# One scale per token instead of scaled copies: the norms of cross attention and router, and the last additions

## What is computed

```python
x = _layernorm(x + _L0_attn_ref(x, ...))        # rotary self attention, softmax and linear memory mixed by a gate
x = _layernorm(x + _L0_xattn_ref(x, ctx, ...))  # cross attention on 64 context tokens
x = _layernorm(x + _L0_ffn_ref(x, ...))         # 64 experts, 8 per token, 64 slots each
# inside the cross attention:
x = rmsnorm(hidden_states, norm_w)              # x * rsqrt(mean(x*x) + 1e-6) * norm_w
q = x @ wq.T
attn = softmax(q k^T * HD**-0.5)                # HD = 16, masked context tokens left out
out = (attn v) @ wo.T
return sigmoid(x @ wg.T) * out
# inside the experts:
probs = softmax(x @ gate_w.T); w, sel = top_k(probs, 8)
```

## Time and profile before

| | us |
|---|---|
| median of 3 runs (453.71 to 455.42) | 454.6 |
| the profiled execution | 454.77 |
| its span in the trace | 453.0 |
| PE busy, share of the span | 292.5 (65%) |
| DVE busy | 226.3 (50%) |
| POOL busy | 168.8 (37%) |
| ACT busy | 129.3 (29%) |

### The profile page before, as it was taken

The page is one execution under the profiler, slowest core; times in us unless marked ns, Lnnn a source line. Parts: engine busy times, 40 slices in busy tenths (PEclk is TensorE's granted clock), DMA queues, the critical chain, the costliest instruction groups (busy, mean ns, idle before and its releaser), DMA issues.

```text
span 453.0 us, 5276 instructions
## 1 busy us (share of the span) xinstructions
PE 292.5 (65%) x1732; PEld 184.2 (41%) x1732; DVE 226.3 (50%) x509; ACT 129.3 (29%) x238; POOL 168.8 (37%) x172
## 2 busy tenths in 40 slices
PE   4475767598996798977889648730059999760000
PEld 3352534455655466564365424620035545330000
DVE  0826451567447766377713624132037777430694
ACT  1340354116652156531355113100014443230000
POOL 1300030300302762118700067105705568484662
PEclk9885699869999699996999659765569999975555
DMA  7299998980075230572200199200059999955951
GB/s 273 89 181 290 358 386 212 234 286 1 1 163 117 104 127 2 135 144 83 79 2 1 55 275 300 57 23 8 1 161 265 317 225 190 247 64 96 359 200 46
DMA packets 44829, 69.75 MB, mean 154 GB/s; under 512 B 5851, under 2 KB 30041, under 8 KB 44034
## 3 DMA queue, kind: packets, MB, share of 16 engines
q1 hardware_dynamic: 36688, 59.67, 45.3%
q0 software_dynamic: 7680, 9.47, 10.3%
q10 hardware_dynamic: 434, 0.27, 0.3%
HBM read 42.74 MB, written 31.90 MB: 165 GB/s over the span
## 4 chain that ended last, share of the span: by engine, by line
PE 39%; DVE 18%; DMA 17%; issue 10%; ACT 6%; POOL 5%; SPq 2%; POOLq 0%; DVEq 0%; ACTq 0%
PE M L1000 16%; PE O L1000 11%; DMA acc_d<-xp_t,idx_out 9%; PE SA L1000 4%; PE SB L1000 4%; DMA early<-part_d 4%; DVE nmax L741 3%; DVE early L980 3%; POOL xin_d L440 2%; ACT xp_t L555 2%; DMA part_d<-early 2%; PE M L1172 2%; DVE xn L894 2%; SPq L340 1%; PE M L1035 1%
## 5 line engine op out<-in xcount | busy, mean ns | idle before, releaser
L440 POOL DMA_INDIRECT xin_d<-row,idx_slot x64 | 62.9, 983 | 28.8 <-issue 18.8
L484 POOL DMA_INDIRECT acc_d<-xp_t,idx_out x32 | 49.5, 1548 | 35.1 <-DVE idx_out L951 13.4
L466 POOL TENSOR_TENSOR early<-early 128x1024 f32<-128x1024 f32 x4 | 8.5, 2131 | 86.0 <-ACT early L543 86.0
L426 POOL TENSOR_SCALAR rstd<-mv 128x2 f32<-128x2 f32 x8 | 1.8, 222 | 92.5 <-DVE mv L719 92.5
L1000 PE MATMUL O<-probs,early 128*32 128x256 f32 x256 | 32.8, 385 | 4.2 <-ACT probs L533 2.2
L1000 PE MATMUL SA<-early 96*128 96x256 bf16 (+1 forms) x128 | 23.2, 313 | 12.0 <-DMA early<-part_d 5.6
L1000 PE MATMUL SB<-early 96*128 96x256 bf16 (+1 forms) x128 | 23.1, 311 | 5.1 <-DVE nmax L741 4.8
L1330 PE MATMUL O<-con,probs 128*128 128x128 f32 x40 | 9.2, 320 | 26.2 <-DMA probs<-xin_d 26.2
L741 DVE TENSOR_REDUCE nmax<-SB 128x4 f32<-128x1024 f32 x16 | 19.5, 1219 | 10.8 <-PE SB L1000 10.8
L741 DVE TENSOR_REDUCE nmax<-SA 128x4 f32<-128x1024 f32 x16 | 19.5, 1217 | 10.4 <-PE SA L1000 10.4
L1000 PE MATMUL O<-xf,early 128*128 128x256 f32 x64 | 19.5, 462 | 5.3 <-DMA early<-weights 5.3
(11 more groups left out here) (190 smaller groups left out, 649.3 us busy)
## 6 DMA issues: line engine op xcount, KB each, us to landing
gu_sb<-wgu SPq DMA_DIRECT2D x21, 384.0 KB, 7.8
acc_d<-zeros SPq DMA_DIRECT2D x3, 2176.0 KB, 19.7
early<-acc_d SPq DMA_DIRECT2D x24, 256.0 KB, 5.8
xin_d<-zeros SPq DMA_DIRECT2D x1, 5136.0 KB, 24.5
early<-wgu SPq DMA_DIRECT2D x11, 384.0 KB, 11.0
wd_sb<-wd SPq DMA_DIRECT2D x21, 192.0 KB, 8.4
early<-part_d SPq DMA_DIRECT2D x28, 128.0 KB, 7.2
probs<-xin_d SPq DMA_DIRECT2D x20, 160.5 KB, 4.7
```

Of the source, the lines that this page charges most:

```text
L440: nc.gpsimd.indirect_dma_start(xin_d, bass.IndirectOffsetOnAxis(ap=idx_slot[:, t, k:k + 1], axis=0), row[:, t, :], None, bounds_check=SLOT ...
L466: nc.gpsimd.tensor_tensor(rest[:], qk[:], parts[:, :, 0], ALU.subtract).then_inc(S["rest_r"], 1)
L484: nc.gpsimd.indirect_dma_start(acc_d[p % CHAINS], bass.IndirectOffsetOnAxis(ap=idx_out[:, p:p + 1], axis=0), yw[:, p % YRING, :], None, bo ...
```

## The change

The scaled copies go. PE transposes `res` itself, before any norm: for cross attention instead of `xn`, for the router instead of `row`. What the norm would have done is put elsewhere:

- The mean: once, at the end of the first iteration, a new `folded` multiplies `w_xq` and `w_xg` by the norm weight and subtracts from them and from the router weights their column mean, which PE forms with a matrix of 1/256 (`mean_of`).
- The scale: POOL makes three scales per token in `nrm` (for the router, for the exponential with the factor 1/4, for the tanh with the factor 1/2), two more adds and one power of six columns. ACT takes them as the scale of its exponentials and of the tanh, which becomes two instructions. For the router DVE multiplies the maximum by `rstd` (`lbias`).
- `x1` is still written for the residual, now behind `score_max(0)`; the rows are written in a new `rows`, behind `router_max`.
- The final stage: POOL's addition goes. DVE adds three parts to three in one instruction of 768 columns, then two of 256; the steps of three tiles are interleaved. ACT does the normalisation (Identity with scale and bias), DVE makes its bias (`fshift`).

```diff
-        rstd = sb("rstd", [P, NT])
+        nrm = sb("nrm", [P, 3, NT])
+        rstd = nrm[:, 0]
+        mean_of = sb("mean_of", [P, P])
         x1 = sb("x1", [P, NT, D])
-        sq = sb("sq", [P, NT, D])
-        ssum = sb("ssum", [P, NT])
-        rinv = sb("rinv", [P, NT])
-        xn = sb("xn", [P, NT, D])
-        xn_f = sb("xn_f", [P, NC, T])
+        x1_f = sb("x1_f", [P, NC, T])
...
+            nc.gpsimd.memset(mean_of[:], 1.0 / D).then_inc(S["setup"], 1)
...
-                passed(pool)
-                nc.gpsimd.tensor_scalar(rstd[:], mv[:, :, 1], 1e-5, None, ALU.add).then_inc(S["var"], 1)
-                need(pool, "var", b, ln)
-                nc.gpsimd.tensor_tensor(rstd[:], rstd[:], mhalf[:, 0:NT], ALU.pow).then_inc(S["rstd"], 1)
+                    prev(pool, "xexp", b)
+                    prev(pool, "eprob", b)
+                    nc.gpsimd.tensor_scalar(nrm[:, 1], mv[:, :, 1], HD * (1.0 + 1e-6), HD * 1e-11, ALU.mult, ALU.add
+                                            ).then_inc(S["var"], 1)
+                    nc.gpsimd.tensor_scalar(nrm[:, 2], mv[:, :, 1], 4.0 * (1.0 + 1e-6), 4e-11, ALU.mult, ALU.add
+                                            ).then_inc(S["var"], 1)
+                nc.gpsimd.tensor_scalar(rstd, mv[:, :, 1], 1e-5, None, ALU.add).then_inc(S["var"], 1)
+                need(pool, "var", b, 2 + ln)
+                if ln == 1:
+                    nc.gpsimd.tensor_tensor(nrm[:].rearrange("p k t -> p (k t)"), nrm[:].rearrange("p k t -> p (k t)"),
+                                            mhalf[:, 0:3 * NT], ALU.pow).then_inc(S["rstd"], 1)
+                else:
+                    nc.gpsimd.tensor_tensor(rstd, rstd, mhalf[:, 0:NT], ALU.pow).then_inc(S["rstd"], 1)
...
-                    need(pool, "sq", b)
-                    prev(pool, "xn", b)
-                    passed(pool)
-                    nc.gpsimd.tensor_scalar(rinv[:], ssum[:], 1.0 / D, 1e-6, ALU.mult, ALU.add).then_inc(S["ssum"], 1)
-                    need(pool, "ssum", b)
-                    nc.gpsimd.tensor_tensor(rinv[:], rinv[:], mhalf[:, 0:NT], ALU.pow).then_inc(S["rinv"], 1)
...
-            def final_half(t):
-                pool.wait_ge(S["gu"][t], fin_base[t] + 16 * CHAINS)
-                by_two = fin[:, t].rearrange("p (c h) d -> p c h d", h=2)
-                nc.gpsimd.tensor_tensor(by_two[:, 1:, 0], by_two[:, 1:, 0], by_two[:, 1:, 1], ALU.add).then_inc(S["fpool"], 1)
-            final_half(0)
             for t in range(TILES):
-                if t + 1 < TILES:
-                    final_half(t + 1)
                 pool.wait_ge(S["fmv"], t + 1)
-                nc.gpsimd.tensor_scalar(rstd[:, t % 2:t % 2 + 1], mv[:, t % 2, 1:2], 1e-5, None, ALU.add).then_inc(S["fvar"], 1)
+                nc.gpsimd.tensor_scalar(frstd[:, t:t + 1], fmv[:, t, 1:2], 1e-5, None, ALU.add).then_inc(S["fvar"], 1)
                 pool.wait_ge(S["fvar"], t + 1)
-                nc.gpsimd.tensor_tensor(rstd[:, t % 2:t % 2 + 1], rstd[:, t % 2:t % 2 + 1], mhalf[:, 0:1],
-                                        ALU.pow).then_inc(S["frstd"], 1)
+                nc.gpsimd.tensor_tensor(frstd[:, t:t + 1], frstd[:, t:t + 1], mhalf[:, 0:1], ALU.pow).then_inc(S["frstd"], 1)
...
-                    nc.scalar.activation(xp[:, t], xp[:, t], ACT.Exp, scale=HD ** -0.5).then_inc(S["xexp"], 1)
+                    nc.scalar.activation(xp[:, t], xp[:, t], ACT.Exp, scale=nrm[:, 1, t:t + 1]).then_inc(S["xexp"], 1)
...
-                    need(act, "lmax", b)
+                    need(act, "lbias", b)
+                    need(act, "rstd", b)
                     for t in range(NT):
                         nc.scalar.activation(eprob[:, t], M[:, 1, t * E:(t + 1) * E], ACT.Exp,
-                                             bias=lmax[:, t:t + 1]).then_inc(S["eprob"], 1)
...
-                        nc.scalar.activation(sq[:, t], x1[:, t], ACT.Square, accum_out=ssum[:, t:t + 1]).then_inc(S["sq"], 1)
-                    need(act, "xn_mm", b)
-                    for n in range(NC):
-                        nc.scalar.activation(xn_f[:, n], M[:, 0, n * T:(n + 1) * T], ACT.Copy,
-                                             scale=par[:, NH + n:NH + n + 1]).then_inc(S["xn_ev"], 1)
+                                             bias=lbias[:, t:t + 1], scale=nrm[:, 0, t:t + 1]).then_inc(S["eprob"], 1)
+                if b is not None:
+                    need(act, "x1_mm", b)
+                    nc.scalar.activation(x1_f[:].rearrange("p c t -> p (c t)"), M[:, 0, :], ACT.Copy).then_inc(S["x1_ev"], 1)
...
-                    nc.scalar.activation(sgate[:].rearrange("p t d -> p (t d)"), gate_place(a), ACT.Tanh, scale=0.5
-                                         ).then_inc(S["gate_th"], 1)
+                    need(act, "rstd", b, 1)
+                    for t in range(NT):
+                        nc.scalar.activation(sgate[:, t], gate_place(a)[:, t * D:(t + 1) * D], ACT.Tanh, scale=nrm[:, 2, t:t + 1]
+                                             ).then_inc(S["gate_th"], 1)
...
+            for t in range(TILES):
+                act.wait_ge(S["fshift"], t + 1)
+                act.wait_ge(S["frstd"], t + 1)
+                nc.scalar.activation(fin[:, t, 0], fin[:, t, 0], ACT.Identity, scale=frstd[:, t:t + 1], bias=fshift[:, t:t + 1]
+                                     ).then_inc(S["fout"], 1)
...
+            def folded():
+                dve.wait_ge(S["w_in"], 16 * 7)
+                dve.wait_ge(S["par_in"], 16)
+                for w in ("xq", "xg"):
+                    for c in range(NC):
+                        nc.vector.tensor_scalar(w_sb[w][:, c], w_sb[w][:, c], par[:, NH + c:NH + c + 1], None, ALU.mult
+                                                ).then_inc(S["fold"], 1)
+                dve.wait_ge(S["fold"], 2 * NC)
+                dve.wait_ge(S["fold_mm"], 1)
+                for i, w in enumerate(("xq", "xg")):
+                    nc.vector.tensor_tensor(w_sb[w][:], w_sb[w][:], M[:, 1, i * D:(i + 1) * D].unsqueeze(1).broadcast_to([P, NC, D]),
+                                            ALU.subtract).then_inc(S["fold"], 1)
+                nc.vector.tensor_tensor(router_sb[:], router_sb[:], M[:, 0, 0:E].unsqueeze(1).broadcast_to([P, NC, E]),
+                                        ALU.subtract).then_inc(S["fold"], 1)
...
+                    statistics(b, 2)
+                def rows():
...
-                    statistics(b, 2)
                     normalized(b, 2, row, "x2")
...
+                    need(dve, "lmax", b)
+                    need(dve, "rstd", b)
+                    nc.vector.tensor_tensor(lbias[:], lmax[:], rstd, ALU.mult).then_inc(S["lbias"], 1)
...
+                if a is not None:
+                    score_max(0)
                 if b is not None:
                     normalized(b, 1, x1, "x1")
-                if a is not None:
-                    score_max(0)
-                if b is not None:
-                    need(dve, "rinv", b)
-                    prev(dve, "xn_mm", b)
-                    for t in range(NT):
-                        nc.vector.tensor_scalar(xn[:, t], x1[:, t], rinv[:, t:t + 1], None, ALU.mult).then_inc(S["xn"], 1)
...
                 if b is not None:
                     router_max()
+                    rows()
                     route()
                 if a is not None:
...
+                if b is None and a is None:
+                    folded()
...
-            def total(t):
+            def halves_added(t):
                 dve.wait_ge(S["gu"][t], fin_base[t] + 16 * CHAINS)
-                f = fin[:, t]
-                nc.vector.tensor_tensor(f[:, 0], f[:, 0], f[:, 1], ALU.add).then_inc(S["fadd"], 1)
-                dve.wait_ge(S["fpool"], t + 1)
-                for c in range(1, CHAINS):
-                    dve.wait_ge(S["fadd"], CHAINS * t + c)
-                    nc.vector.tensor_tensor(f[:, 0], f[:, 0], f[:, 2 * c], ALU.add).then_inc(S["fadd"], 1)
-                dve.wait_ge(S["fadd"], CHAINS * (t + 1))
-                nc.vector.bn_stats(stats[:, t % 2], f[:, 0]).then_inc(S["fstat"], 1)
+                nc.vector.tensor_tensor(fin[:, t, 0:3], fin[:, t, 0:3], fin[:, t, 3:6], ALU.add).then_inc(S["fpair"], 1)
+            def thirds_added(t, c):
+                dve.wait_ge(S["fpair"], t + 1)
+                if c == 2:
+                    dve.wait_ge(S["fadd"], 2 * t + 1)
+                nc.vector.tensor_tensor(fin[:, t, 0], fin[:, t, 0], fin[:, t, c], ALU.add).then_inc(S["fadd"], 1)
...
+            def row_stats(t):
+                dve.wait_ge(S["fadd"], 2 * t + 2)
+                nc.vector.bn_stats(fstats[:, t], fin[:, t, 0]).then_inc(S["fstat"], 1)
...
-                nc.vector.bn_aggr(mv[:, t % 2], stats[:, t % 2]).then_inc(S["fmv"], 1)
...
+                nc.vector.bn_aggr(fmv[:, t], fstats[:, t]).then_inc(S["fmv"], 1)
...
-                nc.vector.tensor_scalar(fin[:, t, 0], fin[:, t, 0], mv[:, t % 2, 0:1], rstd[:, t % 2:t % 2 + 1],
```

(37 more changed lines are left out.)

41 lines of the change are left out of this document (22 added, 19 removed).

## The result

| | before | after |
|---|---|---|
| median, us | 455.01 (4 runs, 453.71 to 455.72) | 438.67 (4 runs, 436.04 to 443.70) |
| ratio | | 0.9615, 95% interval 0.9567 to 0.9663 |
| profiled execution, span | 454.77, 453.0 | 443.70, 441.9 |
| batch 3's first residual to its `idx_slot` | 50.8 | 48.9 |
| first addition to last normalisation | 26.1 | 21.4 |

The change makes the kernel 3.9% faster. The forecast of 436.2 was 2.5 us low; the range (430.5 to 443.0) holds the median. The trace of after is that of the slowest of its four runs, which the ratio leaves out: it shows 11.1 us of gain in the span where the forecast had 18.6 and the median 16.3. A run of 437.3, that of half_scatters (experiment 6), is put beside it further down.

What follows compares the result with a forecast made beforehand. It took the last iteration's chain through every norm step, and DVE at borders and final stage, as the bound. 1.0 - 2.6 - 8.7 + 0.3 - 4.2 - 4.4 = -18.6, from 454.77 to 436.2 us; range 430.5 to 443.0.

Steps and rivals of the forecast that it cites:

- beginning, to the first maximum: First iteration: `folded`'s work on PE and DVE outlasts a transfer wait and delays the first maximum; +1.0 us.
- borders, to batch 3's first residual: Three borders with self attention beside: DVE sets the pace and writes `x1` in place of `xn`; -2.6 us.
- last iteration, front, to the scores: Last iteration, residual to context scores: PE at the full clock, POOL's `xk_blk` arriving last; -8.7 us.
- behind the scores, to the second residual: Last iteration, ACT: the tanh becomes two instructions, with the exponentials behind it on the path; +0.3 us.
- router, to `route`: Last iteration, second residual to `route`: PE starts at once, at the full clock; -4.2 us.
- experts, to the first addition: Experts' stage, 305 to 421 us: not touched, only starting earlier by what is won before; 0.
- final stage, to the last normalisation: Final stage: without POOL's addition a tile costs DVE 2.4 us, before 3.26; -4.4 us.
- The first rival: Borders: PE's clock stays high once its wait for `xn` is gone; 431.7 us in all, chance 0.13.
- fourth rival: New pauses keep PE at 1.2 GHz; slower than before from 18.6 us of such work, 473 at twice that; chance 0.04.

Runs made afterwards that it cites:

- experiment 6: Changed kernel with every second of POOL's 16 scatters of the first three batches left out: 437.9 us (436.3 to 444.6), ratio 0.9623.
- pval_again: Changed kernel with PE's wait for `pval` moved behind the transposes, in a series where the kernel before took 475.1: 451.9 us, ratio 0.9505.
- pval_calm: Changed kernel with PE's wait for `pval` moved behind the transposes, in an undisturbed series: 437.3 us (434.9 to 440.4), ratio 0.9636.
- filled_calm: pval_calm plus a few matmuls nobody reads in PE's pauses of the last iteration, same series: 431.1 us (430.5 to 433.8), ratio 0.9504.
- the two disturbed series: First two of four measurement series, everything 4% longer: the kernel before took 474.4 and 475.1 us, against 454.5 and 454.4 in the last two.

## Why the prediction was right, and where not

The sum was -18.6, the median's gain 16.3. The terms, by two traces: that of after (a run of 443.7) and that of half_scatters (a run of 437.3, the same kernel but for half of the scatters of the first three batches). Change against before, us:

| term | forecast | run of 443.7 | run of 437.3 |
|---|---|---|---|
| beginning, to the first maximum | +1.0 | +1.18 | +0.86 |
| borders, to batch 3's first residual | -2.6 | -4.39 | -3.30 |
| last iteration, front, to the scores | -8.7 | -5.88 | -6.43 |
| behind the scores, to the second residual | +0.3 | +7.79 | +0.35 |
| router, to `route` | -4.2 | -3.83 | -3.54 |
| experts, to the first addition | 0 | -0.86 | +0.72 |
| final stage, to the last normalisation | -4.4 | -4.67 | -6.32 |
| end | 0 | -0.44 | +0.16 |
| sum | -18.6 | -11.1 | -17.5 |

- *Beginning.* The work of `folded` was hidden in after and cost 0.4 in pval_again. Its matmuls took 0.55 + 1.08 + 1.03 in after and not the 4.8 of the low clock, because the clock was up. The first maximum is nevertheless 1.18 later than before: the operands landed later (38.30 against 37.12), as did everything since the first transfers. That is not the change, so the +1.0 was met by accident.
- *Borders.* First to second maximum shrank from 3.49, 4.06, 4.06 to 3.00, 3.00, 3.01: -2.6, as forecast. Another 1.8 in after is mostly the last output projection of self attention, which ran at 1.2 GHz before (3.78) and at 2.4 in this run (1.99). The forecast had no term for that, and in half_scatters it took 3.78 again. The first rival's clock came in part: the border projections took 2.59, 2.88 and 3.17 (before 3.62, 3.62 and 3.33). It was worth little: in pval_calm they took 3.62 each, and the second and third stretch from residual to residual 57.96 and 57.16, against 57.72 and 56.93 in after.
- *Last iteration, front.* Two steps failed. First, I removed the wait for `xn` and didn't ask what else the transposes wait for: `prev("pval")`, over some 5 us before `xn` was, now came last, 2.0 behind the residual. Second, I took the full clock, from a stretch in which it was 0.97 with PE idle; that the clock is up in a pause says nothing about the work behind it. The projection took 3.78 (3.67 in half_scatters) and the gap from residual to scores was 8.35 (7.80). The prediction had named a projection of 3.8 and a gap over 7 as signs that it was wrong, and in this place it was.
- *Behind the scores.* ACT's part is the +0.3 of the forecast (tanh 0.84 for 0.60, exponentials 0.09 more each), and it is all that the run of 437.3 shows. The other 7.5 of the run of 443.7 are the clock, from rows at either level: 3.2 up to the gate, 1.0 at the transposes of the weights, 3.3 at the weighted values. This is the fourth rival's mechanism (work that turns low costs as much again), in one place and at 7.5 us instead of 18.6: I had given it 0.04 as a slower kernel, and should have carried it as a bound of this term. Why the clock fell ahead of the weighted values in one run and behind them in the other isn't known.
- *Router.* The matmuls ran partly at the low clock (1.50 for 0.99), and ACT's two exponentials, 0.70 for 0.52, came behind a maximum and `lbias` that took 0.5.
- *Final stage.* The term was too small, which the waiting second tile hides in after. A tile takes 2.17 and not 2.4, since the instructions of 256 columns follow each other 0.33 to 0.35 apart, not 0.42. In after the second tile lost 1.6 waiting for its transfer, which I had excluded only for the last one. ACT's Identity is 0.60, not 0.5.
- Small: POOL's power of six columns took 1.34 (1.2). What the experts' stage did in the two traces was not followed up.

So the number came out well in part by luck. In the run of 437.3 the front, the router and the experts gave 3.7 less than forecast, and the final stage and the stretch over the borders 2.6 more. The terms on DVE at the borders and on the order of work at the router were right to some tenths; the places where PE is the path were sized by a clock that the kernel gets in some runs only. With the wait moved and the clock held up (filled_calm), the front gives 14.23 - 5.58 = 8.65, the 8.7 of the forecast.

## What to carry over

When a wait goes, list everything else that the released instruction waits for, also what was long over: here a reuse of PSUM came last, and only its order had to be changed. Where TensorE alone is the path and stops for a microsecond or two at each step, its clock is a term of the sum with two values. Filler matmuls that mostly end before the real work is due turned runs of 434.9 to 440.4 into 430.5 to 433.8 here; they cost when they stick out, and in the two disturbed series they didn't help. Price a filler by a row of the same form first.
